# Load order, key tiles and row statistics in the order of use, and the first output's largest values and turned pieces elsewhere in VectorE's order, in a fused cross-attention and feed-forward kernel

## What is computed

```python
def _dyn_quant(x):                       # rows to whole numbers of -127..127
    s = maximum(max(abs(x), axis=-1) / 127.0, 1e-8)
    return clip(round(x / s), -127, 127), s

xa = layernorm(x)
q  = w8a8_linear(xa, wq, bq)             # both sides quantised, bf16 products are exact
k  = cond @ wk.T + bk;  v = cond @ wv.T + bv        # fp32
o  = softmax(q @ k.T / sqrt(32) + mask) @ v         # 16 heads
x1 = x + w8a8_linear(o, wo, bo)          # needs the largest |o| of each of the 512 rows
g, u = qlinear(layernorm(x1), w_gate), qlinear(layernorm(x1), w_up)
out = x1 + qlinear(silu(g) * u, w_down)
```

## Time and profile before

| what | value |
|---|---|
| median of three runs | 477.38 us (476.62 to 478.38) |
| the profiled execution's own time | 477.79 us |
| its span, first to last instruction | 476.0 us |
| granted TensorE clock | 1.00 of full speed in all 40 slices |
| busy PE / DVE / ACT / POOL | 98% / 77% / 55% / 50% of the span |
| chain that ended last, by engine | PE 77%, DVE 13%, DMA 4%, ACT 3%, issue 2% |
| DMA in all | 77.41 MB, mean 163 GB/s |

### The profile page before, as it was taken

The page is one execution under the profiler, slowest core; times in us unless marked ns, Lnnn a source line. Parts: engine busy times, 40 slices in busy tenths (PEclk is TensorE's granted clock), DMA queues, the critical chain, the costliest instruction groups (busy, mean ns, idle before and its releaser), DMA issues.

```text
span 476.0 us, 6950 instructions
## 1 busy us (share of the span) xinstructions
PE 465.8 (98%) x2390; PEld 302.0 (63%) x2390; DVE 365.0 (77%) x486; ACT 261.9 (55%) x465; POOL 238.5 (50%) x131
## 2 busy tenths in 40 slices
PE   8999899999999999999999999999999999999996
PEld 5888588677654454545454454534468778888885
DVE  3589888897988798978879898789966468574325
ACT  3586987321567576666756796667824223222220
POOL 3004211912489888787978878787022122222230
PEclk9999999999999999999999999999999999999999
DMA  5999997998677928091642800030244424446322
GB/s 181 319 313 393 372 280 283 303 275 329 139 197 163 298 72 178 2 211 33 139 106 64 181 2 1 1 133 2 67 154 134 134 78 155 157 133 229 132 68 91
DMA packets 44390, 77.41 MB, mean 163 GB/s; under 512 B 5281, under 2 KB 13505, under 8 KB 44353
## 3 DMA queue, kind: packets, MB, share of 16 engines
q1 hardware_dynamic: 44064, 76.41, 54.3%
q10 hardware_dynamic: 288, 0.52, 0.3%
HBM read 57.95 MB, written 18.87 MB: 161 GB/s over the span
## 4 chain that ended last, share of the span: by engine, by line
PE 77%; DVE 13%; DMA 4%; ACT 3%; issue 2%; SPq 0%; DVEq 0%; ACTq 0%
PE ps L881 13%; PE ps L903 12%; PE ps L853 12%; PE ps L778 8%; PE ps L779 8%; PE ps L990 4%; PE ps L991 4%; PE ps L802 3%; DVE neg_m L1444 3%; PE ps L690 2%; PE ps L692 2%; PE ps L691 2%; DMA raw<-in_ctx_t 2%; PE ps L813 2%; DVE kq_lo L1418 1%
## 5 line engine op out<-in xcount | busy, mean ns | idle before, releaser
L1444 DVE TENSOR_REDUCE neg_m<-ps 128x1 f32<-128x1024 f32 x128 | 149.7, 1216 | 23.4 <-PE ps L853 23.4
L1193 ACT ACTIVATE p_t<-ps 128x512 f32<-128x512 f32 x256 | 137.6, 597 | 43.9 <-PE ps L881 40.4
L1777 POOL TENSOR_TENSOR p_sum<-p_sum,p_t 128x1024 f32<-128x1024 f32 x44 | 105.5, 2410 | 3.2 <-ACT p_t L1193 0.8
L881 PE MATMUL ps<-q_st,k_st 97*128 97x512 f32 x256 | 93.5, 425 | 1.0 <-ACT p_t L1193 0.9
L1777 POOL TENSOR_TENSOR p_sum<-p_t 128x1024 f32<-128x1024 f32 x29 | 70.1, 2419 | 30.0 <-ACT p_t L1193 16.3
L853 PE MATMUL ps<-k_st,q_st 96*128 96x512 f32 x256 | 83.3, 407 | 0.8 <-DVE neg_m L1444 0.4
L881 PEld LDWEIGHTS ps<-q_st,k_st 97*128 97x128 f32 x256 | 47.5, 188 | 51.2 <-ACT p_t L1193 37.3
L778 PE MATMUL ps<-xt_hi,k_st 128*128 128x512 f32 x176 | 68.9, 391 | 0.0
L779 PE MATMUL ps<-xt_lo,k_st 128*128 128x512 f32 x176 | 68.6, 390 | 0.0
L903 PE MATMUL ps<-p_t,v_gr 128*32 128x512 f32 x512 | 68.2, 604 | 0.1
L1721 POOL TENSOR_TENSOR v_st<-v_st,bv_bc 128x512 f32<-128x512 f32 x16 | 20.1, 1286 | 88.8 <-DVE qin L1389 35.0
(11 more groups left out here) (143 smaller groups left out, 664.0 us busy)
## 6 DMA issues: line engine op xcount, KB each, us to landing
k_st<-k_hi_d SPq DMA_DIRECT2D x16, 512.0 KB, 6.9
mask_sb<-in_mask SPq DMA_DIRECT2D x3, 2048.0 KB, 13.2
w_int<-in_w_gate SPq DMA_DIRECT2D x22, 256.0 KB, 2.6
w_int<-in_w_up SPq DMA_DIRECT2D x22, 256.0 KB, 2.9
w_int<-in_w_down SPq DMA_DIRECT2D x22, 256.0 KB, 3.6
k_hi_d<-kq_hi SPq DMA_DIRECT2D x16, 256.0 KB, 6.7
k_lo_d<-kq_lo SPq DMA_DIRECT2D x16, 256.0 KB, 7.4
v_d<-v_st SPq DMA_DIRECT2D x16, 256.0 KB, 10.9
```

The costliest lines, as they stand in the source:

```text
L881: mm = pe.matmul(ps[:, bank, :], k_st[g % SLOTS][0:rows, j, P * lc:P * lc + P], q_st[g % SLOTS][0:rows, j, :], start=True, stop=not with_mask)
L1193: act.activation(p_t[:, q % 4, j, :], ps[:, score_bank(q, j), :], ACT.Exp).then_inc(exp_done, 1)
L1444: dve.tensor_reduce(neg_m[:, g % 2, nt, j:j + 1], ps[:, bank:bank + 2, :], AX_XY, ALU.max, negate=True).then_inc(max_read, 1)
L1777: pool.tensor_tensor(total, former, p_t[:, q % 4, hs, :], ALU.add).then_inc(added_pool, 1)
```

## The change

SP's loads: the first rows of x come before the context chunks of item 3 and these before wq; the second rows of x before the biases. The store of V 0 is moved ahead of the load of wo. ACT and DVE: all first chunks, then K 0, then the first half's statistics, then wq's steps; rounding of wq after the second statistics; the second `inverse_std` after the scaled queries. The rounding of wo is moved ahead of the mask flag and of `split_lo` of item 5. In attention, the largest values of the first output come from two reductions over the first three groups' columns (two tiles each, 128x768 values, at (4, 2) and (4, 4)) and at (4, 6) one over the last group's columns (128x512) with a `tensor_tensor` maximum of 128x4 values in SBUF; and the tail's pieces come before `add(q - 2)` in a step.

```diff
@@ -85,6 +85,7 @@
...
         qmx = sb("qmx", [P, 6, NT], F32)
+        qmx_parts = sb("qmx_parts", [P, 2, NT], F32)
         qsc = sb("qsc", [P, 6, NT], F32)
...
@@ -363,7 +364,8 @@
...
-        LARGEST_AT = {(OT, 5): 0, (OT, 6): 1, (OT, 7): 2, (OT + 1, 0): 3}
+        LARGEST_AT = {(OT, 2): (0, 1), (OT, 4): (2, 3)}
+        LARGEST_OVER = (OT, 6)
         SCALE_LC = 2
...
@@ -499,18 +501,17 @@
...
             load_chunks(range(0, RAW, 2))
-            load_chunks(range(RAW, 10))
+            load_chunks(range(RAW, 12))
             sp.dma_start(bk_c[:, :], bk).then_inc(d_kq_bias, 16)
             sp.dma_start(bq_c[:, :], bq).then_inc(d_kq_bias, 16)
+            load_x(0)
+            load_chunks(chunks_of(3))
             sp.dma_start(w_row, wq.rearrange("(t p) c -> p t c", p=P)).then_inc(d_w_row, 16)
-            load_chunks(range(10, 12))
-            load_x(0)
+            load_x(1)
             sp.dma_start(bv_bc[:, :], bv.partition_broadcast(P)).then_inc(d_bias, 16)
...
             sp.dma_start(sup[:, :], s_up).then_inc(d_bias, 16)
-            load_chunks(chunks_of(3))
-            load_x(1)
...
@@ -571,10 +572,10 @@
...
             load_mask(1)
+            store_v(0)
...
             sp.dma_start(w_row, wo.rearrange("(t p) c -> p t c", p=P)).then_inc(d_w_row, 16)
-            store_v(0)
             store_kq("K", 1)
...
@@ -1142,16 +1143,17 @@
...
             kq_tiles("K", 0)
-            scale_set(WQ_SET)
-            split_hi(chunks_of(3))
+            split_hi(chunks_of(3)[:2])
+            centre(0)
+            std(0)
+            split_hi(chunks_of(3)[2:])
             act.wait_ge(d_bias, 4 * 16)
             v_tiles(0)
-            centre(0)
-            std(0)
+            scale_set(WQ_SET)
             scale_set(X_SET)
             kq_tiles("K", 1)
+            split_hi(chunks_of(4))
             std(1)
-            split_hi(chunks_of(4))
             sum_mask(1)
...
@@ -1366,9 +1368,21 @@
...
-            def largest_of_output(t):
-                dve.tensor_reduce(qmx[:, O_SET, t:t + 1], o_sb[:, t, :], AX_X, ALU.max,
+            def largest_of_former_groups(tiles):
+                dve.wait_ge(o_done, OT - 1)
+                rows = slice(tiles[0], tiles[-1] + 1)
+                dve.tensor_reduce(qmx_parts[:, 0, rows], o_sb[:, rows, 0:C - P], AX_X, ALU.max,
                                   apply_absolute_value=True).then_inc(o_largest, 1)
+            def largest_of_output():
+                dve.wait_ge(o_done, OT)
+                then(dve.tensor_reduce(qmx_parts[:, 1, :], o_sb[:, 0:NT, C - P:C], AX_X, ALU.max,
+                                       apply_absolute_value=True))
+                dve.wait_ge(o_largest, len(LARGEST_AT))
+                dve.tensor_tensor(qmx[:, O_SET, :], qmx_parts[:, 0, :], qmx_parts[:, 1, :],
+                                  ALU.max).then_inc(o_largest, 1)
...
@@ -1445,37 +1459,36 @@
...
             dve.memset(qb_a[:, 0, 0, :], 1.0).then_inc(idle_operands, 1)
-            split_lo(range(10))
-            dve.wait_ge(d_w_row, 16)
-            steps(WQ_SET, w_row)
-            split_lo(range(10, 12))
+            split_lo(range(12))
             dve.wait_ge(d_kq_bias, 2 * 16)
...
                 k_tile(0, j)
-            split_lo(chunks_of(3)[:2])
             dve.wait_ge(d_x[0], 16)
...
             mean_and_variance(0)
+            split_lo(chunks_of(3)[:2])
+            dve.wait_ge(d_w_row, 16)
+            steps(WQ_SET, w_row)
             split_lo(chunks_of(3)[2:])
-            dve.wait_ge(d_bias, 4 * 16)
-            round_rows(WQ_SET, w_row, qb_a[:, 0, :, :], None)
             inverse_std(0)
             steps_of_rows(0)
+            dve.wait_ge(d_bias, 4 * 16)
             dve.tensor_scalar(swq[:, :], qsc[:, WQ_SET, :], INV_SQRT_D, None, ALU.mult)
...
             mean_and_variance(1)
+            round_rows(WQ_SET, w_row, qb_a[:, 0, :, :], None)
             round_rows(X_SET, y_a, qb_a[:, 1, :, :], None)
...
             split_lo(chunks_of(4))
-            inverse_std(1)
             copy_turned("T", 0, 0, wq_t)
...
                 q_scaled_tile(0, j)
+            inverse_std(1)
             steps_of_rows(1)
...
@@ -1490,11 +1503,11 @@
...
             round_rows(X_SET + 1, y_a, qb_a[:, 0, :, :], ("T", 0, 3))
+            round_rows(WO_SET, w_row, qb_a[:, 1, :, :], ("T", 1, 3))
             bank = content(("F", 0, 0))
...
             split_lo(chunks_of(5))
-            round_rows(WO_SET, w_row, qb_a[:, 1, :, :], ("T", 1, 3))
             copy_turned("T", 2, 2, qx_t)
...
@@ -1603,16 +1616,16 @@
...
                         normalise_output(g - 1)
-                    if quad(g, lc) >= 2:
-                        add(quad(g, lc) - 2)
                     for key in tail:
...
                             tail_part(0, key[1], key[2] + k, bank)
+                    if quad(g, lc) >= 2:
+                        add(quad(g, lc) - 2)
                     if (g, lc) in LARGEST_AT:
-                        dve.wait_ge(o_done, OT)
-                        largest_of_output(LARGEST_AT[g, lc])
+                        largest_of_former_groups(LARGEST_AT[g, lc])
+                    elif (g, lc) == LARGEST_OVER:
+                        largest_of_output()
                     elif (g, lc) == (OT + 1, 1):
...
@@ -1752,7 +1765,7 @@
...
-                    pool.wait_ge(o_largest, NT)
+                    pool.wait_ge(o_largest, len(LARGEST_AT) + 1)
                     pool.tensor_scalar(qsc[:, O_SET, :], qmx[:, O_SET, :], 1.0 / QMAX, QUANT_EPS,
...
                 if q == 2 * SET + 1:
```

## The result

The changed kernel takes 491.36 us (median of six runs, 489.31 to 492.68), the kernel before 477.13 beside it (476.37 to 478.38): a ratio of 1.0295 [1.0274, 1.0316], 14.2 us slower. The direction was forecast; 487.2 was 4.2 us too low, and the result lies 0.9 us above the range. The profiled execution took 489.31 us with a span of 487.4, so it is 2 us shorter than the median.

The account below looks back on a forecast made before the run. PE, busy 98% of the span, was taken as the bound. Terms 2.05 + 1.7 - 0.6 + 6.7 = +9.85 us on the profiled 477.79 gave 487.6, stated as 487.2 for a median 0.4 lower; range 477.5 to 490.5.

Parts of the forecast that it names:

- loads, statistics: First 56 us: Q gains 1.1 us as ACT then waits only for the mask, swallowed by the later DVE delay.
- rounding of wo first: 76 to 88 us: POOL starts early, its adds alternate with DVE's four low parts, scaled queries come later: +2.05 us.
- largest values, (4, 6): At (4, 6) the two-input maximum of 128x4 values waits for POOL's running add, delaying PE: +1.7 us.
- pieces first at (6, 1): At (6, 1) turned pieces are copied while the add was held anyway, so PE's wait goes: -0.6 us.
- wait at the sums of group 6: From (6, 5): late add delays POOL, whose adds hold the inverse deviation's small operations; sums wait for q = 55: +6.7 us.
- (7, 3) and (7, 4): An add comes some 1.3 us later, with slack in the exponentials: at most 0.3 us.
- all three places: Low parts near 78 us, maximum at (4, 6), small operations at (6, 5): DVE held by POOL's adds; chance 0.62.
- Rival A: Only wide operations and `tensor_scalar` are held, four-value two-input ones slip in: +1.8, 479.2, up to 482.5; chance 0.19.
- rival B: POOL's adds do not alternate with DVE's queued operations, small chains slip: -1.7, 475.7, or 474.5; chance 0.14.
- rival C: Loads come worse than thought (x late or a chunk behind wq): +1 to +3 on top, 489 to 490.5; chance 0.05.

Follow-up runs that it names:

- whole front: Kernel before with only the change's first stage (loads, key tiles, statistics, rounding of wo): 478.26 us, ratio 1.0036.
- both edits: Changed kernel with 22 idle PE products before the late add at the sums of group 6, and the add first at (7, 3) and (7, 4): 484.91 us.
- the last chip: Changed kernel unedited, run again beside its version with idle products and the add first in group 7: 491.11 us; kernel before there 476.64.
- the first part of the third batch: Kernel before with the change's loads, key tiles, statistics and store of V 0, rounding of wo left where it was: 476.48 us, ratio 0.9982.
- the third batch: Runs beside the kernel before (476.82 us, 33 runs): the front in two parts, pieces first at (6, 1) alone, and the changed kernel with its costly places mended.
- the three versions that were level or faster: Kernel before with new loads and statistics, 476.48 us; with pieces first at (6, 1) alone, 476.03; changed kernel with its three costly places mended, 476.04.
- the changed kernel with three mends: Changed kernel with add first except at (6, 1), last maximum as tensor_reduce, POOL's third bias_v held until the low parts are done: 476.04 us, ratio 0.9976.

## Why the forecast was right and where it failed

| step | forecast | measured |
|---|---|---|
| loads, statistics | 1.1 swallowed | -0.3 of 476.8, not told from 0 |
| rounding of wo first | +2.05 | +2.0 (alone; 1.6 by the ratio), +1.6 (whole front) |
| largest values, (4, 6) | +1.7 | +1.7 (trace): 1.2 the `tensor_tensor`, 0.5 the new places |
| pieces first at (6, 1) | -0.6 | -0.7 (trace), -0.8 (alone) |
| wait at the sums of group 6 | +6.7 | +5.2 (its halves start 6.1 us apart, 0.9 before) |
| (7, 3) and (7, 4) | at most 0.3 | +2.3 |
| the clock | not a term | +3.9 (both edits less the wait); by rows 1.6 to 2.5 and 1.4 to 1.65 |

With 1.8 for the front, between its two values, the column is 1.8 + 1.7 - 0.7 + 5.2 + 2.3 + 3.9 = 14.2, as measured (14.5 on the last chip); that it fits to the tenth is chance, since several terms are known only to some tenths. Without the clock it is 10.3, 487.4.

**Right.** The direction, and the mechanism of all three places: a DVE instruction with two SBUF inputs is held to the end of POOL's running add, even if it has four values a row. (`ve`, a `tensor_scalar` with one SBUF input, was held too, 1.53 us for 0.79.) Rival A (only wide ones are held) falls with the 2.03 of the maximum and the 2.28, 2.29 and 2.19 of the small ones; rival B (no alternation) with the 6.65 of the low parts; rival C with the first part of the third batch. By the rule of the Trainium skill that the forecast weighed (SBUF — State Buffer, Who interferes with whom), such an instruction contends with a GpSimd instruction that reads SBUF and `tensor_reduce` never does on trn2; the trace agrees: the `tensor_tensor` took 2.03 us beside POOL, the same maximum as a reduction 0.16. The +1.7 at (4, 6) is right in size partly by luck: the held maximum cost 1.2, and 0.5 came from the new places, which the forecast had at nothing.

**Wrong, the sum.** First and largest, the granted clock had no term at all. The profile of before showed 1.00 in all slices, with no wait of PE over 1.4 us; a forecast that makes PE stand still for 5 us leaves that state, and I carried the 1.00 over. The runs put 3.9 us in its place. Second, "At (7, 3) and (7, 4) an add comes some 1.3 us later, with slack in the exponentials: at most 0.3". It cost 2.3. I had counted the length of the pieces, not what they wait for: DVE idled 5.31 us for ACT's `xt_hi`, which waits for PE's turned tiles. At (6, 5) I had seen and priced just this. What waits for the add was missed too, the exponentials that write over its inputs, and the slack: before, the add ended 0.1 us ahead of them. Third, the step "`sums` ... starts there: +6.7", too much by 1.5. The 331.0 was counted along the profile of before; with PE 1.5 us late from further up (325.86 against 324.36) it stands for 332.5. The add ended at 331.9, 0.6 sooner, because three small operations, not seven, were left behind the last held one. And `sums` has two halves, of which only the second waits: 0.9 us of it run before. 6.7 - 0.6 - 0.9 = 5.2.

With the clock's 3.9 the forecast's sum would have been 13.75, right to 0.5 us. That is luck in part: one error of 1.5 too much stands against one of 2.3 too little.

**A reading that misled.** The profile of before is one execution, and a late one in the first stage. By it the new loads brought Q 1.6 us forward and the front as a whole cost 0.5 us; against the other executions the front costs about 2. It was not only the mask that was late. With the old order of loads ACT reached the mask after its landing in all four profiles: at 45.42, 45.98, 47.26 and 48.11, behind landings at 44.96 to 46.4. In the profile of before ACT had waited 1.71 us for a context chunk until 29.62 (1.04 us until 27.78 in the one with 45.42), and its list stayed 1.84 us behind from there. With the new order ACT waits 1.7 to 2.6 us for the mask in all twelve profiles. So the forecast's mechanism there, a list of ACT that is no longer the last to come, is seen; what it gains depends on how late the list would have been, and the time of the whole kernel shows no gain that stands clear of nothing.

**Open.** Of before's 33 runs in the third batch six took over 478 us (up to 480.39), and none of the 33 runs of the three versions that were level or faster. Whether the new order of loads, or a few tenths elsewhere, spares PE such a late execution, these runs can't say: the version with only (6, 1) changed has the old loads and has none either. At what length of a wait the clock falls was not tried, and the length alone does not decide: it fell behind waits of 1.55 and 2.2 us and in five of seven profiles behind the 2.3 us at (7, 4), and did not behind 1.9 and 2.1. The 1.9 us of `issue` before the second queries have no releaser in the trace; they went when POOL was held back, so they probably belong to the low parts. Why the changed kernel with three mends is 0.7 us better than the sum of its terms is open too.

## What to carry to other kernels

Before an operation is moved ahead of another on one engine's list, look at what it waits for, not only at how long it runs: the add behind it inherits that wait, and so does everyone who waits for the add's result or for its input buffer. Small two-input DVE operations in a dependent chain belong where POOL rests, or in a form that is not held (a reduction over both parts cost 0.16 us where the `tensor_tensor` cost 2.03). When a forecast makes PE stand for microseconds, add a term for the clock behind the wait; and read a second execution of the kernel before, before a landing time or a late list enters a sum.

## What the runs showed of the hardware

- After PE had stood still from 326.9 the granted clock was 0.50 from 331 to 337 us, also behind the end of the wait, and with 22 idle products in the same gap it stayed at 1.00. Behind the wait of 2.3 us it fell in five profiles and stayed in two of the changed kernel. The same products took 1.6 to 2.5 us longer behind the first wait where it fell, 1.4 to 1.65 behind the second.
- The mask of 2 MB landed at 44.96 us in one and at 46.4 in another profile of kernels with the same order of loads. Q started at 54.07 and at 57.40: ACT's list was 2.7 us later in the second, and PE's clock was 0.50 just before Q.
- In the alternation both engines pay: POOL's four bias adds took 6.32 us beside DVE's low parts, 4.94 without.
